# Masking every second head of the second attention on VectorE behind the exponential, with a new order of instructions

## What is computed

```python
x = x + attention0(norm(x), ctx)        # 16 heads of 16, softmax
x = x + one_of_8_experts(norm(x))       # argmax gate
x = x + attention1(norm(x), ctx)        # 16 heads of 16, with a fixed mask of allowed (i, j)
x = x + coupling_net(norm(x))           # 3 cycles of Gelu layers
x = x + linear_attention(norm(x), ctx)
x = x + lora_experts(norm(x))
x = x + attention3(norm(x), ctx, mask)  # one head
x = x + gated_mlp(norm(x))
```

```python
scores = jnp.einsum('bhqd,bhkd->bhqk', q, k) * SCALE
scores = jnp.where(mask, scores, jnp.finfo(scores.dtype).min)
attn = jax.nn.softmax(scores, axis=-1)
```

## Time and profile before

| | us |
|---|---|
| median of 3 runs | 1091.88 (1087.68 to 1097.86) |
| profiled execution | 1095.82 |
| its span, first to last instruction | 1094.0 |
| mean granted TensorE clock | 0.975 |

### The profile page before, as it was taken

The page is one execution under the profiler, slowest core; times in us unless marked ns, Lnnn a source line. Parts: engine busy times, 40 slices in busy tenths (PEclk is TensorE's granted clock), DMA queues, the critical chain, the costliest instruction groups (busy, mean ns, idle before and its releaser), DMA issues.

```text
span 1094.0 us, 17887 instructions
## 1 busy us (share of the span) xinstructions
PE 1027.3 (94%) x6322; PEld 700.0 (64%) x6322; DVE 646.5 (59%) x2246; ACT 510.1 (47%) x1091; POOL 220.6 (20%) x314
## 2 busy tenths in 40 slices
PE   7699999888999999999999999999999999999988
PEld 5365664555567765767576756776666756667767
DVE  4245673657667565666667565766667555535553
ACT  1050543465247542574247533574366343765311
POOL 2021330214030220313030222213121112001200
PEclk9599999989999999999999999999999999999999
DMA  7426630324022220403121230412041003000000
GB/s 230 47 52 185 174 83 6 63 45 88 21 47 52 53 46 20 97 10 78 30 57 42 54 63 2 98 43 56 1 86 27 11 7 75 4 10 1 1 10 11
DMA packets 43175, 57.07 MB, mean 52 GB/s; under 512 B 4488, under 2 KB 39056, under 8 KB 39568
## 3 DMA queue, kind: packets, MB, share of 16 engines
q1 hardware_dynamic: 40880, 47.16, 20.1%
q10 hardware_dynamic: 2208, 8.78, 2.6%
HBM read 40.19 MB, written 13.89 MB: 49 GB/s over the span
## 4 chain that ended last, share of the span: by engine, by line
PE 79%; ACT 7%; DMA 4%; DVE 4%; issue 3%; SPq 1%; POOL 1%; ACTq 0%; DVEq 0%
PE bank L1614 11%; PE bank L1947 7%; PE bank L1465 6%; PE bank L1474 6%; PE bank L1674 5%; PE bank L1696 5%; PE bank L1958 4%; PE bank L1731 4%; PE bank L1586 4%; PE bank L1967 3%; DMA QA<-negm 2%; PE bank L1725 2%; PE bank L1677 2%; PE bank L1483 2%; PE bank L1908 1%
## 5 line engine op out<-in xcount | busy, mean ns | idle before, releaser
L855 ACT ACTIVATE PT<-bank 128x512 f32<-128x512 f32 x256 | 153.0, 598 | 194.4 <-PE bank L1677 131.2
L1614 PE MATMUL bank<-w,xhT 128*128 128x512 f32 x256 | 129.0, 610 | 0.0
L1674 PE MATMUL bank<-QA,KA 98*128 98x256 bf16 x512 | 116.1, 280 | 10.7 <-ACT PT L855 7.4
L1153 DVE CUSTOM_DVE_ANT_0 bank<-bank,maskb 128x256 f32<-128x256 f32 x256 | 102.3, 451 | 33.5 <-PE bank L1586 33.1
L1146 DVE TENSOR_REDUCE mx<-bank 128x2 f32<-128x512 f32 x128 | 83.7, 683 | 39.8 <-PE bank L1586 39.3
L1586 PE MATMUL bank<-KA,QA 96*128 96x256 bf16 x512 | 90.9, 279 | 12.6 <-DMA QA<-qparts 8.9
L1198 DVE SCALAR_TENSOR_TENSOR x<-bank,one,x 128x256 f32<-128x256 f32 x128 | 61.8, 483 | 61.1 <-PE bank L1614 58.4
L1947 PE MATMUL bank<-xhBT,wi 128*128 128x256 f32 x336 | 86.7, 391 | 5.2 <-DVE hT L1450 5.1
L1674 PEld LDWEIGHTS bank<-QA,KA 98*128 98x128 bf16 x512 | 46.0, 100 | 68.0 <-ACT PT L855 36.9
L1696 PE MATMUL bank<-PT,vaug 128*32 128x256 f32 x1024 | 72.7, 393 | 3.0 <-ACT PT L855 3.0
L1586 PEld LDWEIGHTS bank<-KA,QA 96*128 96x128 bf16 x512 | 45.7, 100 | 39.3 <-issue 14.8
(11 more groups left out here) (310 smaller groups left out, 2013.0 us busy)
## 6 DMA issues: line engine op xcount, KB each, us to landing
QA<-scratch SPq DMA_DIRECT2D x90, 128.0 KB, 4.3
scratch<-kparts SPq DMA_DIRECT2D x30, 192.0 KB, 2.3
KA<-scratch SPq DMA_DIRECT2D x15, 384.0 KB, 4.5
scratch<-qparts SPq DMA_DIRECT2D x30, 192.0 KB, 2.3
KA<-scratch SPq DMA_DIRECT2D x15, 256.0 KB, 5.2
wi<-ipack ACTq DMA_DIRECT2D x1, 2304.0 KB, 8.5
w<-pack ACTq DMA_DIRECT2D x1, 2169.0 KB, 14.5
xin<-x_in SPq DMA_DIRECT2D x8, 256.0 KB, 3.2
```

The source lines that it names most:

```text
L855: act.activation(PT[:, n % RING, :, :].rearrange("p t s -> p (t s)"), st_bank[:, :], ACT.Exp).then_inc(exp_s, 1)
L1153: last = dve.tensor_tensor_reduce(s, s, maskb[:, t, :], op0=ALU.add, op1=ALU.max, scale=1.0, scalar=-HUGE, accum_out=mx[:, i % 4, n % GH, ...
L1614: last = pe.matmul(bank[n % 2][:, :], xhT[:, kk, t * P:(t + 1) * P], W("exp0", KT)[:, kk, i * 512:(i + 1) * 512], start=(kk == 0), stop=(k ...
L1674: last = pe.matmul(st_bank[:, t * S:(t + 1) * S], KA[m][0:KM, v, t * P:(t + 1) * P], QA[m][0:KM, v, :], start=True, stop=(m == 0))
```

## The change

Of the 16 heads of each second attention, the even ones lose the two mask matmuls. They are exponentiated without the mask (their row maximum is still that of the allowed pairs). VectorE then goes over the head's PT in one scalar_tensor_tensor of 128x512: min(maskb + 2^127, PT). OFF becomes -2^127, so that this is 0 where the pair isn't allowed and PT elsewhere. The product with the values waits for these too (live_s, 8 a second attention). The odd heads are masked by TensorE as before. On VectorE the new instructions of a group stand one group ahead of the division of the group before.

All five strings of TURNS are new. The numbers of turns stay the same for each thread, but for 64 more v turns on VectorE, 7 more w (135) and 8 more z (92) on TensorE. The strings of the other engines but ScalarE are cut from the diff here.

```diff
@@ -29,7 +29,7 @@
 HID = 768
 HT = HID // P
 EPS = 1e-5
-OFF = -1.0e30
+OFF = -2.0 ** 127
 RING = 8
 HUGE = 3.0e38
...
     "scalar":
-        "ppppppppppppvppvpvvvvpvvvvvvvvvvvvvvvvvvvpspssbspssbbppbvvvvvbvbbbbbbbbbbbvbvvvvvbbbbvbvvvvvpvpvpvvv"
-        "pvpvvvvvpvsvvvvvvvvvvvvvvvvvvvvpassapavapavpvvvavvavvvvvapavavvvvvavpvpvvvavpavaavpvvvvvavavvvsvvpvb"
-        "vvbvvvpvvbvvvvvbsbsbapappvababvavvvbvavbvvvvvvbvavbpvvavavabvpvvvapvvaavababvpvvvpavavvvvvvsvvbvpbvv"
-        "vvvvvpbvvvbsbsbapappvababvavvvbvavbvvvvvvbvavbpvvavavabvpvvvapvvaavababvpvvvpavavvvvvvsvvbvpbvvvvvvv"
-        "pbvvvbsbsbapappvababvavvvbvavbvvvvvvbvavbpvvavavabvpvvvapvvaavababvpvvvpavavvvvvsvvvbpvbvvvvpvbvvvvv"
-        "bsbsbapappvababvavvvvbvvvvvvbapvvvvvbavavbvavvvabpvpavpavaabavbvvpvsvavavvvvvvbvbvvvvvvvbvvvspvsbpab"
-        "vbapvpvvpvavbvavvbvvvapbpvvvvvbvvvavvavbavabvabaavasavabvvvbvvavvavvvvvvbvvvbvsvvvsvbvvcbabbavaabavb"
-        "vvvvbavvavbvavvavabvvvvabvavbavavvavvvbaabaaaaaabaaaabaaaaaaaaabaaaaaaaaaaabbaabaabcbcccbbbcbcbccccc"
-        "ccccccccccccccc",
+        "pppppppppppppvpvvvvvvpvvvvvpvvvvvvvvvvvvpvspsspppbsssbpbppvbppbbbbvbbvvbbvbbvbbvbbvvbvvbvbbvvvvvvvvv"
+        "vvvvvpsvvvvvvvvvvvvvvvvvvvvvvvpvsspaavppaavavvvvavavvavvavapvvvvvavppvavavvavapvpvaavsvpvvvvbvvvbvvv"
+        "vvvvvpvbvvvvvvbvsbsbapappvababvavvbvavvbvvavvavbavpavvvvbvavvbavvavavbappvbpvpavavvvvvsvbvvvbvvvvvvv"
+        "bvvpvvvvpbvsbsbapappvababvavvbvavvbvvavvavbavpavvvvbvavvbavvavavbappvbpvpavavvvvvsvbvvvbvvvvvvvbvvpv"
+        "vvvpbvsbsbapappvababvavvbvavvbvvavvavbavpavvvvbvavvbavvavavbappvbpvpavavvvvvsvbvvbvvvvvvvvbvvpvvvvpb"
+        "vsbsbapappvababvavvbvvavvvbavvavbavpabvvvvavvvbavvavavpapvbpbpvaavsvvvvvvbvpbvvvvvvvvvpbvvvvsvvsbvpp"
+        "bvpbavavvbvavavbavvpvvbvavpvvvvbvavavbavvavbvavbaaavasvbvvbvavavvvvvvvvbvbvvvvvvvvbvvssbcabbaaababaa"
+        "vbaavbavvvvbvavavbvvavavabvvvvvvvvvvvabavbaaaaaaaaaabaabaaaaaaaabaaaaaaaaababaabaabccccbccbccbcccbcc"
+        "bcccccbcccccccc",
...
@@ -326,6 +327,9 @@
         def at(L, name, b, n, h=0):
             return nth(L.s[name], b, n) if L.t == "b" else STEP[name, n, h]
 
+        def cut_later(v):
+            return v % 2 == 0
+
         def net_bank(h):
             return bank[1] if h else la
 
@@ -366,7 +370,7 @@
         s_ps, max_s = sem("s_ps"), sem("max_s")
         mq_s, mT_ps, negm_s = sem("mq_s"), sem("mT_ps"), sem("negm_s")
         m_rows = [sem(f"m_rows{i}") for i in range(2)]
-        st_ps, exp_s = sem("st_ps"), sem("exp_s")
+        st_ps, exp_s, live_s = sem("st_ps"), sem("exp_s"), sem("live_s")
         pv_ps, ot_s, otT_ps, att_s = sem("pv_ps"), sem("ot_s"), sem("otT_ps"), sem("att_s")
         attT_ps, attT_s, o_ps, added = sem("attT_ps"), sem("attT_s"), sem("o_ps"), sem("added")
 
@@ -1221,6 +1225,15 @@
                 dve.tensor_tensor(dst[:, lo:hi, :].rearrange("p t d -> p (t d)"), ps[:, lo * D:hi * D],
                                   src[:, lo:hi, :].rearrange("p t d -> p (t d)"), ALU.add).then_inc(done, 1)
 
+            def only_live(q, g):
+                for v in range(g * GH, (g + 1) * GH):
+                    if cut_later(v):
+                        n = q * H + v
+                        dve.wait_ge(exp_s, n + 1)
+                        p = PT[:, n % RING, :, :]
+                        dve.scalar_tensor_tensor(p, maskb[:, :, :], -OFF, p, ALU.add, ALU.min).then_inc(live_s, 1)
+                        yield
+
             def value():
                 dve.memset(KA[0][KR:KM, :, :], 1.0).then_inc(mask_ready, 1)
                 yield
@@ -1232,7 +1245,11 @@
                 last.then_inc(mask_ready, 1)
                 yield
                 for q, (b, m) in enumerate(ATTENTIONS):
+                    if m == 1:
+                        yield from only_live(q, 0)
                     for g in range(ITEMS):
+                        if m == 1 and g + 1 < ITEMS:
+                            yield from only_live(q, g + 1)
                         i = q * ITEMS + g
                         dve.wait_ge(otT_ps, i + 1)
                         if g == 0 and q:
@@ -1672,8 +1689,8 @@
                                 pe.wait_ge(exp_s, n)
                             for t in range(T):
                                 last = pe.matmul(st_bank[:, t * S:(t + 1) * S], KA[m][0:KM, v, t * P:(t + 1) * P],
-                                                 QA[m][0:KM, v, :], start=True, stop=(m == 0))
-                                if m == 1:
+                                                 QA[m][0:KM, v, :], start=True, stop=(m == 0 or cut_later(v)))
+                                if m == 1 and not cut_later(v):
                                     last = pe.matmul(st_bank[:, t * S:(t + 1) * S], identb[:, :], maskb[:, t, :],
                                                      start=False, stop=True)
                             last.then_inc(st_ps, 1)
@@ -1685,6 +1702,8 @@
                             g = (v - 5) // GH
                             i = q * ITEMS + g
                             pe.wait_ge(exp_s, GH * (i + 1))
+                            if m == 1:
+                                pe.wait_ge(live_s, (b * ITEMS + g + 1) * sum(map(cut_later, range(GH))))
                             if i:
                                 pe.wait_ge(ot_s, i)
                             if g == 0:
```

More of the change, by code:

```diff
@@ L84 @@
     "sync":
-        "bpppppvvpvvpppppppppsvpsssvpppvvpppppvpppvvvppsvsssvppppvvppppvpvpppvvppbsssvsbpvpppvvpppvbpvpvpppvp"
-        "pbsssvsbpvpppvvpppvbpvpvpppvppbsssvsbpvpppvvpppvbpvpvpppvppbsssvsbpvpppvvppppvbvpvpppppvsbsssvvpbppp"
-        "vvpcvbvvvpppssssbvbvvvbbcc",
+        "bpppppvpvvvpppppppppppppsvpsssvvvppppppvpvvvppsvssspvpppvvpppppvpppvvvppbssvssbpvpppvvbvpppppvpppvvp"
+        "pbssvssbpvpppvvbvpppppvpppvvppbssvssbpvpppvvbvpppppvpppvvppbssvssbpvpppvvbppvpppppvpppvvsbsssvppppbv"
@@ L88 @@
+        "vvpcvbvvvpppbssssbvvvvbbcc",
     "gpsimd":
-        "ppppppppppssssssppppppppssassssppppppppaassbbbsasssbppppppaappssbbbsasssbppppppaappssbbbsasssbpppppp"
-        "aappssbbbsasssbppppppsaasppbbsbssasbppppssaabbsssbsabaaaabbbaaaabcccccccc",
+        "ppppppppppsssppsssppppppsssasssppppppaappssbbbsasssbppppaappppsbbsbsasssbppppaappppsbbsbsasssbppppaa"
+        "ppppsbbsbsasssbppppppaapspsbbsbsssappbppssaabbsbasssbaaaabbbaaaabcccccccc",
     "scalar":
-        "ppppppppppppvppvpvvvvpvvvvvvvvvvvvvvvvvvvpspssbspssbbppbvvvvvbvbbbbbbbbbbbvbvvvvvbbbbvbvvvvvpvpvpvvv"
@@ new lines @@
+    "tensor":
+        "pwwppwwwwpwwwppppwwwwwwwwwwwwwwwpwwwpwwpwwwwpwwpsspswspsspvswswswswwwwswswvswsvvwwwvwsvswwwwwwwwvpwv"
+        "vvvpvpvwwwvwpvvvvpvvwwwwwwvwwwvvvwwwvvwvwwvwpvwwwvvpwwpswwwssspsssssssssssssspwwppbspsspbbsspbspssps"
+        "bvbsswwbbpswsppsswswspvspvvsbvvwwwwwsvswwvvvsvswwvsvswwvwwwvvvvssvvswwwsvwwvvvsswvvsvswvwwswvwwsvvww"
+        "wwwvwwwpwswwwsvsvvsvsvssvsvvvvsvvssvsvvvvsvvssvsvvvsvvsvpvpvswvvssppwwssapssaasspvssasspavsspassvvsv"
+        "vasavavvvpassvsassvvsassvspvvvvassvpvavasspvvsavssavvavpvpvapvvapvapsvsvvsvsvsbsvbvvvvssvvsvsvvvvpvs"
+        "vbsvbsvvbsvssvsvvsvpbvbvvbspssabpssbbaapsspavsspbsabsbvasspbvvbvssavbavbvvvavsbsbsasspvvsassvsbavvvv"
+        "bvavsspvbavbvavbbbabvvsbbasspvbavsbvsbpvvbbsvpspavpasspvvbavvvsvbvvsbvssvsvvsvsspvvsvsvvssbvsbvvbsvs"
+        "svsvvsvpbpvbvvbspssabpssbbaapsspavsspbsabsbvasspbvvbvssavbavbvvvavsbsbsasspvvsassvsbavvvvbvavsspvbav"
+        "bvavbbbabvvsbbasspvbavsbvsbpvvbbsvpspavpasspvvbavvvsvbvvsbvssvsvvsvsspvvsvsvvssbvsbvvbsvssvsvvsvpbpv"
+        "bvvbspssabpssbbaapsspavsspbsabsbvasspbvvbvssavbavbvvvavsbsbsasspvvsassvsbavvvvbvavsspvbavbvavbbbabvv"
+        "sbbasspvbavsbvsbpvvbbsvpspavpasspvvbavvvsvbvsvbvssvsvvsvssvvsvsvvpsbsvbsvsvbsvsvsvvsvpbvpbvvbspssabp"
+        "ssbbaapsspavsspbsabsbvssapsbvvsbvssvasvavbvsbvasvspbbassvvsasvsbabvvvvssavpvbvavvbavsspbbasvbvsbabsv"
+        "bavssbvpvvbbppbvbppabavsavsvssvpvssvssvbsvvbsvssvsvvsvssvvsvsvvpbvpbvvbvsvvpsvsvpbvssbvvbssppssvsbsa"
+        "pbbsavsavvspsabsvsbvbsspasspvsassvvvsvbbvavvsavvvbvbvavsvbbsaspvvssapsvsbabsvsvvvavabvbavbbabavbabbs"
+        "vssbvvsbbvsabvabvsavbvvvsvvsvsvsbvvbsvssvsvvsvsvsvsvvbbbvvvsvvssbccbbaccababbcaabassbbssasaabvbsassa"
+        "bvbassvvsvvbbvavsaasbbvvvasbbvvssazvzzazzvvvvbvvbbvbvvvbvvbvabvavbvvabzzzzbbaazzaaaabzaazaazzzaabbaz"
+        "zaaaaazzzzzzzzazaazaazazzzzbzzbaabaaaaazaazaabazbbzzzzzzzzzzazazzzbaabbzzzzaazzzzzzzbczcccbbzzzzzzcz"
+        "zzzzzzzzzzcccbbbccbccbcbccczzzzzzzzzzzbcbcccccbccccbccccbccccbccccbccccbcbcbcccc",
```

39 lines of the change are left out of this document (11 added, 28 removed).

## The result

The changed kernel takes 1114.34 us in the median (1110.0 to 1116.53), against 1093.22 us of the kernel before measured with it: a ratio of 1.0217, 95% interval 1.0166 to 1.0267. The forecast was 1088 us with a range to 1106 us. The kernel is slower by 21 us, and the time lies beyond the range. The profiled execution spans 1113.3 us (1094.0 before), and its mean granted clock is 0.956 (0.975 before).

A forecast was written before the change was run, and what follows sets the result against it. TensorE was taken as the bound (busy 94%, 79% of the chain). Masks -13.4, fillers +1, Gelu blocks +8.7 and VectorE 0 sum to -3.7 us: 1091.9 - 3.7 = 1088 us, 8-in-10 range 1075 to 1106.

The forecast's parts named there:

- The masks removed, -13.4 us: TensorE, second attentions: 128 of 256 mask matmuls go, 14.1 us by issue spacing or 12.6 by chain share; middle taken.
- VectorE's 64 instructions, cost 0: Second attentions: 64 x 0.69 = 44 us more VectorE work, covered by its idle time, so 0 on the path.
- The third rival: VectorE's queue holds TensorE up: each new instruction puts 0.35 us on the chain, 22 us, 1101 us; chance 0.07.
- The meeting with GpSimd: Some 13 of VectorE's 64 new instructions would meet GpSimd's work, losing up to 0.7 us each, 9 us of VectorE time.
- Fillers, +1 us: TensorE: 15 more spins of two blank matmuls, between 0 and 3.3 us; +1 us taken.
- The Gelu blocks, +8.7 us: ScalarE, first attentions: 6.5 more blocks alternating Exp and Gelu with table loads, each idling TensorE 1.34 us.
- the slower rival of 1109 us: First attention of each round: second Gelu block becomes a ScalarE stretch, 4.6 us per block, 30 us; chance 0.15.
- the sign that I had named: The Gelu block term is wrong if the ScalarE pieces of the chain (table loads) don't grow.
- The DMAs issued per thread are the same in number. ... No term.: SP's and GpSimd's orders shift a few turns; waits for the maxima's rows, 22.8 us of chain, may move either way.
- I give the clock no term.: TensorE, 160 to 974 us: granted clock is 0.98, nearly always the upper level, 2.4 GHz, so no cost counted.
- the second rival: The slower rival of 1109 us: second Gelu block as a ScalarE stretch, 30 us; chance 0.15.
- The whole would be wrong if the stretch between the first and the last mask matmul moved by more than 14 us while none of these rows did: Sign against the whole forecast; the rows are the predicted counts, busy times and chain shares.

The follow-up runs named there:

- e4: The kernel before with the two mask matmuls of every even head left out and nothing in their place (output incomplete); it gained 11 us (8 to 14).

## Why the prediction was wrong, step by step

*The masks removed, -13.4 us.* Right in mechanism and, within its interval, in size: e4 measured -11 us (8 to 14). Of the two ways to price them, the share of the chain (12.6 us) was the nearer.

*VectorE's 64 instructions, cost 0.* The duration was right: 0.69 us forecast, the row says

```profile
L1234 DVE SCALAR_TENSOR_TENSOR PT<-maskb,PT x64: 658/691/1757, 162.0 to 995.7; 128x512 f32<-128x512 bf16 x64
```

with a median of 691 ns. The cover was not whole: about 4 us come back in the old order, 0.06 us a piece. In the changed kernel the product waited for a mask twice, 1.7 us, although it was head 2's and not head 3's: both times VectorE's queue had other work ahead of it. The third rival's 22 us did not come. The meeting with GpSimd is visible, but 3 times and not the 13 that I had estimated: of the three instructions that start at 522.19 and take 2.95 us, the first takes 1.75 us beside a GpSimd instruction, the other two 0.68 us each (VectorE's timeline, then GpSimd's):

```profile
522.19 2.95 DVE L1234 SCALAR_TENSOR_TENSOR PT<-maskb,PT 128x512 f32<-128x512 bf16 x3
```

```profile
522.08 1.31 POOL L671 TENSOR_TENSOR x<-x,xh 128x512 f32<-128x512 f32 x1
```

*Fillers, +1 us.* They were all there, 470. They weren't tested by themselves.

*The Gelu blocks, +8.7 us, and the slower rival of 1109 us.* The count of loads and ScalarE's busy time (536 forecast, 535.6) were exact, the conclusion was wrong. The old order pays as much for its 74 loads as the new for its 94. The sign that I had named didn't help: ScalarE's share of the chain did grow, from 7% to 10%, and yet the loads aren't the loss. That the rival's 1109 us lies near the measured 1114 is chance: its mechanism isn't what happened.

*"The DMAs issued per thread are the same in number. ... No term."* This is the step that failed, together with its wider form, that each thread has the same number of turns, and so a new order has no price of its own. Same number doesn't mean same place. I walked the ScalarE string turn by turn and never walked TensorE's, although the chain said that TensorE is 79% of it. What had to be asked was: in which stretch does TensorE have nothing of its own to do but wait for a serial chain on the other engines, and how much work does each order put there? The old trace held the place, from 501 to 520 us, full of TensorE's work, and I never asked whether the new string keeps that work there. It has 30 TensorE instructions fewer in it, with the masking the same, and VectorE's statistics start behind an addition that they stood ahead of. The order as a whole costs 29 us.

*"I give the clock no term."* That the earlier trace rows shows 0.98 says what the old order keeps up, not what the new one would. Holes in TensorE's work come first, the lower level follows: TensorE was at the lower level for 54.6 us of the run before and for 99.0 us after. The same four matmuls take 1.9 times as long there (below), so the 44.4 us more are worth at most 22 us. The Trainium skill ("TensorE: Matmul & The Clock Gate", section "HAM oscillation — how this bites in real kernels") says that pauses between bursts throw the engine back to its lower clock, and prices the time spent there at one half. The trace agrees on the price: the same four expert matmuls take 3.62 us behind the hole and 1.88 us without one. The pauses ahead of the fall at 521.5 us were short here: 0.69, 0.95 and 0.94 us.

*The range.* Its upper end, 1106, was taken from a part of the second rival. No rival stood for the order itself losing cover, so nothing reached to 1114. "The whole would be wrong if the stretch between the first and the last mask matmul moved by more than 14 us while none of these rows did" is the sentence that came true: that stretch grew by 19.7 us (813.1 to 832.9), the seven rounds by 30.6 us, and the counted rows came out as forecast. Only TensorE's share of the chain didn't: it fell by 5 points instead of 1.

## What to carry to other kernels

When a change rewrites an order by hand, walk the bound engine's queue first, stretch by stretch, and ask at every serial chain on other engines how much of the bound engine's work stands beside it, and whether the chain still starts as soon as its input is there; the total is the same in any order and says nothing. Idle time of the bound engine is paid twice where its clock falls afterwards: in the round shown 4.4 us of added idle time came with 5.3 us of slower work. And measure the parts of a combined change apart: here a gain of 7 us and a loss of 29 us came as one.

## What the runs showed of the hardware

Two of the seven holes in TensorE's work ended in 13.7 us at a granted clock of 0.50, in which the experts' 512-column matmuls started 0.85 us apart instead of 0.43; behind the other five it was 6.8, 6.8, 3.4, 0 and 0 us. Blank matmuls in the hole came with a clock of 1.00 instead of 0.79 in that stretch, and so 24.6 us of useless work on the busiest engine cost 0.9 us between the medians. VectorE's masking instruction, 691 ns in the median, took 1750 to 1757 ns three times of 64. Each of the three started 0.11 us behind a GpSimd instruction that adds x and xh in SBUF (line 671), which agrees with the rule that the prediction quoted from the Trainium skill ("SBUF — State Buffer", section "Who interferes with whom"). Four more overlapped a GpSimd instruction in the trace and took 692 to 694 ns as the others do; why these weren't slowed is open.
